# Writing out the edge stage of a graph network kernel: TensorE, VectorE and SyncE programs without loops

## The reference, cut to what matters

```
x = concatenate([node[src], node[dst], edge_features], -1)      # 200000 x 160
h = relu(x @ W1.T + b1)                                          # the edge network
messages = h @ W2.T + b2
agg = segment_sum(messages, dst, num_segments=6250)
node = gru(agg, node)
```

## Time and profile before

| | |
|---|---|
| median of 3 runs | 5424.33 us (5411.29 to 5428.64) |
| profiled execution | 5421.28 us, its span 5419.5 us |
| edge stage: POOL's first gather to DVE's last message | about 2670 to 5320 us |
| PE, DVE, POOL, ACT busy, share of the span | 62%, 52%, 36%, 17% |
| mean granted TensorE clock | 0.686 of full speed |

### The profile page before, as it was taken

The page is one execution under the profiler, slowest core; times in us unless marked ns, Lnnn a source line. Parts: engine busy times, 40 slices in busy tenths (PEclk is TensorE's granted clock), DMA queues, the critical chain, the costliest instruction groups (busy, mean ns, idle before and its releaser), DMA issues. The chain is left out here.

```text
span 5419.5 us, 89480 instructions
## 1 busy us (share of the span) xinstructions
PE 3373.2 (62%) x24458; PEld 2518.9 (46%) x24459; DVE 2843.3 (52%) x7137; ACT 944.6 (17%) x2120; POOL 1974.9 (36%) x2334
## 2 busy tenths in 40 slices
PE   4526777776979989989624444444544444445456
PEld 3412333333979988989513332333333333333345
DVE  8976887776553411332324444444554444445565
ACT  3521246664011200001100000000000000000002
POOL 4670000000021111111365655656665555555550
PEclk5558998888999999999655555555555555555557
DMA  3000011112524444544212222222222222222220
GB/s 130 2 3 13 25 47 59 59 59 99 197 70 143 148 153 156 186 158 154 77 41 52 54 53 51 54 52 55 58 57 55 53 53 53 53 52 60 57 59 22
DMA packets 173577, 404.19 MB, mean 75 GB/s; under 512 B 47902, under 2 KB 109481, under 8 KB 172809
## 3 DMA queue, kind: packets, MB, share of 16 engines
q1 hardware_dynamic: 52409, 259.35, 13.4%
q10 hardware_dynamic: 69360, 91.59, 6.2%
q0 software_dynamic: 51680, 51.82, 5.4%
HBM read 359.52 MB, written 43.07 MB: 74 GB/s over the span
## 5 line engine op out<-in xcount | busy, mean ns | idle before, releaser
L704 POOL DMA_INDIRECT scr<-ptable,src_i x1566 | 1520.6, 971 | 1086.0 <-POOLq L702 617.8
L1151 PE MATMUL ps_all<-stat_w,scr 128*128 128x392 fp8e4 x2712 | 615.4, 363 | 255.3 <-PEq L1155 147.2
L964 PE MATMUL ps_all<-arena 128*128 (+1 forms) x1854 | 351.8, 363 | 676.5 <-PEq L962 332.2
L673 POOL COPY late<-late 128x256 f32<-128x256 f32 (+1 forms) x65 | 25.9, 398 | 1980.8 <-POOLq L671 1980.8
L975 PE MATMUL ps_all<-arena 128*128 128x192 bf16 x1854 | 382.3, 360 | 524.1 <-issue 380.7
L967 PE MATMUL ps_all<-sb_w_e,arena 64*128 64x128 f32 x1854 | 530.6, 441 | 233.9 <-issue 233.4
L1042 PE MATMUL ps_all<-scr,arena 128*128 128x192 bf16 x7203 | 611.1, 247 | 66.9 <-PEq L1040 66.9
L1042 PEld LDWEIGHTS ps_all<-scr,arena 128*128 128x128 fp8e4 x7203 | 600.1, 98 | 76.7 <-issue 74.8
L964 PEld LDWEIGHTS ps_all<-arena 128*128 128x128 bf16 x1854 | 227.0, 137 | 809.8 <-issue 798.7
L912 ACT ACTIVATE arena<-arena 128x384 f32<-128x384 f32 x309 | 161.6, 523 | 2499.1 <-ACTq L911 2114.0
L975 PEld LDWEIGHTS ps_all<-arena 128*128 128x128 bf16 x1854 | 230.2, 143 | 695.6 <-issue 687.8
(11 more groups left out here) (305 smaller groups left out, 3620.2 us busy)
## 6 DMA issues: line engine op xcount, KB each, us to landing
arena<-a_dram SPq DMA_DIRECT2D x245, 784.0 KB, 4.4
arena<-low_dram ACTq DMA_DIRECT2D x309, 192.0 KB
a_dram<-arena SPq DMA_DIRECT2D x49, 784.0 KB, 3.3
arena<-in_e32g ACTq DMA_DIRECT2D x309, 96.0 KB
scr<-ptable,src_i POOLq DMA_INDIRECT x1566
arena<-in_e16p SPq DMA_DIRECT2D x1, 13387.5 KB, 35.3
x<-in_x_nm SPq DMA_DIRECT2D x1, 1664.0 KB, 8.3
out_nm<-x SPq DMA_DIRECT2D x1, 1664.0 KB
```

What stands on the lines that cost most here:

```text
L704: pool.indirect_dma_start(grow[:, g % RING, j, :], None, ptable, bass.IndirectOffsetOnAxis(ap=src_i[:, g * GC + j:g * GC + j + 1], axis=0) ...
L964: pe.matmul(z[:, j // 2, j % 2 * 3 * H:(j % 2 + 1) * 3 * H], onehotT[:, m, j * P:(j + 1) * P], qsp[:, ds(t, 1), :], start=j % 2 == 0, stop ...
L1151: return pe.matmul(bank_w[i][:, 0:WC], oh_lo[u][:, j, :], oh_hi[u][:, j, :], **{"start": False, "stop": False, **flags})
```

## The change

The loops of PE, DVE and SP in the edge stage are written out. A new helper `each_visit` does what `all_visits` does, without `Fori`; the registers are still loaded once every four visits. SP's groups get numbers known when the program is built, so the register that held the landing count and the address register of `group_tab` turn into constants. Instructions of the visits, waits, buffers, and their order on each engine are the same. ACT keeps its loop, and POOL was written out already.

```diff
+        def each_visit(eng, first, last, visit):
+
+            for n in range(NV):
+                if n % 4 == 0:
+                    four = visits(eng, n // 4, first, last)
+                visit(n, n % 4, *four[n % 4])
+
@@ sync
             def group(g, r, landed):
-                if isinstance(g, int) and not AHEAD <= g < NG - RING + AHEAD:
-                    pass
-                else:
+                if AHEAD <= g < NG - RING + AHEAD:
                     done = sp.value_load(group_tab[0:1, ds(g - AHEAD, 1)], min_val=1, max_val=NV)
                     sp.wait_ge(s_done, done)
                     sp.sem_inc(s_free, 1)
                 sp.wait_ge(s_row[r], landed)
                 sp.sem_inc(s_land, 1)
 
-            for g in range(RING):
-                group(g, g, 16 * GC)
-            with sp.Fori(1, NG // RING) as i:
-                landed = sp.snap((i + 1) * (16 * GC))
-                for r in range(RING):
-                    group(i * RING + r, r, landed)
-            for g in range(NG // RING * RING, NG):
+            for g in range(NG):
                 group(g, g % RING, 16 * GC * (g // RING + 1))
@@ tensor
-                all_visits(pe, 3, 4, visit)
+                each_visit(pe, 3, 4, visit)
@@ vector
-                all_visits(v, 1, 5, visit)
+                each_visit(v, 1, 5, visit)
```

## The result

The changed kernel takes 5441.03 us (median of 10 runs, 5434.46 to 5448.28) against 5423.83 us for the kernel before on the same chip (10 runs, 5409.21 to 5437.13). The ratio is 1.0031, with an interval of 1.0018 to 1.0044: 17 us slower (0.3%, small but outside the noise), where 39 us faster was forecast. The profiled execution took 5446.24 us (span 5444.5).

A forecast was written before the change was run, and what follows sets the result against it. POOL's rate (floor 1989 us) and 75 full-ring stops (617.8 us) from late visits were taken to bound the edge stage. Loop work saved 39 us, packets and SP nothing: 5421.3 - 39 = 5382 us (5385 against the median), range 5090 to 5780.

The forecast's parts named there:

- The slow stretches: Edge-stage periods when PE, DVE and SP sequencers manage one instruction per 0.7 us or worse; claimed to stay without loops.
- 70 to 76 times for 560 to 620 us: How often and how long POOL would still be held at L702 by a full ring, if the forecast was right.
- some 112: Instruction packets added by writing out the edge stage: 56 for DVE, 46 for PE, 10 for SP.
- quick visits of 4.8 us: Three of four edge-stage visits, faster than POOL's 6.4 us per visit; expected to keep their 4.8 us.
- The first rival: Edge-stage loops cause the slow sequencing of PE, DVE and SP; 4803 us in full, 5112 by half; chance 0.15.
- the second: An instruction packet wanted while sequencers are slow costs 20 us; 5701 us for DVE's, 5941 with PE's; chance 0.25.
- Taking packets at nothing: Fetching the written-out edge-stage code was priced at nothing, with bounds of nothing and 520 us.
- The third rival: Cycle of POOL and visits shifts phase, nothing gained by count; 5400 to 5450 us; chance 0.12 together with no effect.
- 19 x 2.1 = 40 us: Saving on PE's and DVE's loop instructions: 19 back-edges in visits of some 20 us, three instructions of 0.7 us each.
- The lower bound: Saving of 0 from the loops' own instructions, if a visit of some 20 us ends with POOL's stop regardless.
- 971 ns per gather: Average time of POOL's 1566 edge-stage gathers, 1520.6 us in sum, used for POOL's floor of 1989 us.
- 13 packets: Instruction packets fetched in the looped part; claimed to show back-edges need no fetch, which would give at least 150.

## Why the prediction was wrong

**What was right.** The slow stretches stay when the loops go: 73 stops and 626.7 us, a little above "70 to 76 times for 560 to 620 us"; 109 packets against some 112; quick visits of 4.8 us; the first visits long from the start of the stage and not from new code (in the changed kernel every visit is new code, and still only the first two wait longer than 23.2 us). The first rival (loops are the cause) and the second (20 us for a packet in a slow stretch) are both out. Taking packets at nothing was right where it could be tested: 124 on SyncE cost 0 us, and with the holds removed the 109 of the change cost nothing on a 4750 chip. The third rival (a shifted phase, 0.12) named the range in which the result fell, but a cycle of ring and visits is not what the runs show; what shifts is single gathers against single operations. The range of 8 in 10 took the result in because it was 690 us wide.

**The step that failed** is "19 x 2.1 = 40 us" for the loop's own instructions in long visits. Nothing of it is to be seen. Where the stops exist, long visits kept their number and length without those instructions (67 over 12 us from ReLU to ReLU, 20.2 on average, against 66 of 19.7, not 75), the stops grew by 8.9 us, and with most of the holds gone in both kernels the changed one is still no faster (5444.91 against 5441.01 us). Where the stops don't exist, writing out SyncE changes the median by -0.5 us, and with the holds removed both kernels need 1965.5 us for the gathers; there the long visits are missing too, so that this half does not test them. The lower bound, "0, if the long visit ends with POOL's stop whatever is in it", fits the runs. Its reason is not shown: I had priced an instruction by its own time in a stretch whose end may be set by other things.

**The term that was missing** decides the sign. I took POOL's 971 ns per gather as a property of the gather. The row beside it read 946/952/1338: a median 19 ns under the mean, 31 us in 139 gathers, which depend on what VectorE does at that moment. They are 39 us in the changed kernel's trace on the 5422 chip. Of the 20.8 us between the traces, 8.1 are these holds, about 4 are the base of a gather (952 to 955 ns, 1566 times; the kernel before has 955 too in one of its traces, so this goes with the execution, not with the change), and 8.9 are stops. That the holds carry the 9 to 12 us of the 4750 chips is shown, by the gathers' times and by removal in both kernels. For the 5422 chips it is shown that the holds follow the same rule. It is not shown how much of the 8.1 us comes with the change and how much with the other base, nor that the stops' 8.9 us belong to the change; so the cause of the 17 us is shown in part.

One argument of the prediction does not stand either. It holds its 13 packets against the rule of the Trainium skill, "Runtime: NRT & Kernel Launch", section "Instruction fetch mechanics". That rule asks for a fetch only when a branch leaves the two resident blocks, and the section gives a block 256 instructions. By an estimate from the prediction's own counts (40 and 24 a visit) a round of four visits has some 160 instructions on TensorE and 96 on VectorE, so the rule asked for no fetch per round, and the 13 packets do not speak against it.

**What stays open.** It is not known why the written-out programs stand worse against the gathers and not better. TensorE's branch took 208 ns once in four visits, and VectorE's round had 186 ns of its own, so the visits' places can move by amounts as large as the part of an operation in which a gather is held (0.2 to 0.4 us). A forecast of the sign would need every gather's start to well under that, and my own forecasts for the delays missed for want of it. Open too are what sets the base to 952 or 955 ns in an execution, and what the slow stretches are. They go with the chip: absent on two, present on three occasions on the others, with loops or without. No run here got at them.

## What to carry to other kernels

Read a steady instruction's minimum, median and maximum, not its mean: where the maximum lies 0.4 us above the median, look at what the other engines do at its start. Where GpSimd's gathers set the pace, a change to VectorE or TensorE that is "hidden" still moves VectorE's operations against them, and 6 to 30 us of 2000 came or went by that alone. A difference of a few us between two single traces is not the effect of a change until the same kernel has been traced twice. And ask for the trace of one more chip before an explanation is built on a stretch that only one chip may have.

## What the runs showed of the hardware

The same kernel takes 4748 to 4761 us on two chips and about 5422 on two others. Of the 661 us between two of its traces all but 30 lie in this one stage. On the slower chips GpSimd stops there for 618 us, and at times SyncE's wait takes 697 to 709 ns where it takes 17 on the others, and its branch 678 ns in the median against 45.

A gather of 0.952 us that starts inside a VectorE operation with two SBUF inputs, or inside the one-hot of the turned rows, ends 0.825 us after that operation. It is not held if it starts ahead of the operation or within its first 0.01 to 0.05 us (0.09 for the one-hot), or beside an addition with one input in PSUM.

The base of a gather is 952 ns in some executions and 955 in others of the same kernel, and the holds of kernels with TensorE's and VectorE's loops were 29 us in two traces at the first and 35 in three at the second (but 35 also in one at the first, with SyncE's added waits).

Waits that pass cost an engine next to nothing while an operation runs ahead of them: 20 instructions before each of GpSimd's 261 groups of gathers, 2 us in all. Two waits in a row share one instruction.

Splitting a VectorE subtraction of 384 elements in two made 2 x 355 ns of 560.
